# One mask for four token tiles, the dt series in portions over two passes, and two end tiles on GpSimd

## The chip, the cores and the metric

The kernel runs on one core of a Trainium2 chip. The core has five engines with an instruction queue each: TensorE (PE, matmuls and transposes), VectorE (DVE), ScalarE (ACT), GpSimd (POOL) and SyncE (SP, which here only issues transfers). They work side by side and wait for each other through semaphores. The metric is the device time of one execution in microseconds (us). PE's clock has two levels, 2.4 and 1.2 GHz; the profile gives the granted clock of a stretch as a share of the higher one.

## The reference

The input is 64 sequences of 32 tokens with 512 channels. Two blocks follow each other, and each adds its result to x.

```python
# block 1: conditional mixing, then a Mamba-2-like attention
att = softmax(mlp(cond))                         # 64 x 8
h   = einsum('boi,bih->boh', att @ weight, x) + (att @ bias_k)[:, :, None]
gate, xBC, dt = split(h @ in_proj_w.T)           # 4096, 6144, 64 columns
x_, B, C = split(silu(causal_conv4(xBC) + conv_bias))
dt  = softplus(dt + dt_bias)                     # 64 heads of 64 channels
state = state * exp(dt * A) + (dt * x_) outer B  # step by step over 32 tokens
y   = state . C + x_ * D                         # 8 heads share one group's B and C
y   = group_rms_norm(y) * norm_weight * silu(gate)
x   = x + y @ out_proj_w.T
# block 2: grouped convolution of 9 taps, then a masked dense layer
z     = conv9(x) + context + bias
hits  = softmax(z @ centroids.T / 0.1) > 0.01
keep  = any(hits, axis=1)[:, None] & any(hits, axis=0)[assignments][None, :]
x     = x + where(keep, z @ ffn_weight.T + ffn_bias, 0)
```

## The kernel before, in words

The 2048 tokens are 16 token tiles of 128, four sequences each. Four token tiles make a block. The scan over 32 tokens is written as products: for each head, Y = (G * L) applied to dt * x, where G is B times C for each pair of tokens of a sequence, and L the decay between them, masked to earlier tokens of the same sequence.

The main loop has 32 stages and a tail (`stage`, n from 0 to 32; L792). A stage is one group of eight heads for one block; even and odd stages alternate between two blocks, and the first 16 stages treat blocks 0 and 1, the last 16 blocks 2 and 3. In a stage ten projections (m from 0 to 9; `proj`, L456) make B (m = 0), C (m = 1), four tiles of x (m = 2 to 5) and four of the gate. A projection is 12 matmuls of 512 columns (L474), since numbers are split into a high and a low part and three products are kept. ACT evicts it from PSUM (`evac`, L479), DVE runs three taps of the causal convolution (`taps`, L501), and ACT the Silu (`silu`, L515). All engines' queues are filled by hand, in the order in which this loop calls the helpers; each engine works its own queue strictly in order. A `wait` in a queue therefore holds up all that is behind it on that engine.

Around the projections stand, on PE's queue:
- `A(n, i)` (L574), for each of the four token tiles i, behind projections 7, 8, 9 and the next stage's 0: four transposes of x (L585) and the product G of that tile (L589, 128 x 128, in the bank PG). A waits for `dtx` of the tile before, because the transposes share one PSUM bank (PT). DVE answers with `A_dve` (L592): `dtx` (L599), and two multiplies of G's diagonal halves by a mask (L607 on, `gmt`), then with `M_dve` (L611), the masked product.
- `Y(n, i)` (L621): 64 short products (L636), tiles 0 and 1 at the end of the stage, 2 and 3 at m = 2 of the next one.
- `O` (L716, matmuls L733) with the output weights and `S` (L697), for the stage before. On the other engines `y_dve`, `y_act`, `y_pool` (L641 to L690) and `add_out` (L738) belong to them.

A new block of tokens comes in at stages 0, 15 and 16 (`block_at`). There the stage also carries, for each of the block's four token tiles, the build of its mixing weights (`X_dve`, L328 to L338, three multiplies on DVE), the product (`X_pe`, L342, L352) and the split into xh (ACT) and xl (DVE, L366), at m = 1 to 4; and behind projection 6 the product that gives dt (`D_pe`, L372). The dt series (`D_chain`, L387) makes softplus of it: four operations and an Exp on ACT (L405 to L410), then 12 short steps on DVE (L412 to L426 and on), each waiting for the one before, on two halves of a PSUM bank and two tiles in SBUF. How many entries of the series are issued at each m is in the tuples `pace0` (stage 0) and `pace` (L780). All of it is issued by the end of the same stage, seven entries at m = 7, six at m = 8, ahead of `A_dve` of these projections' successors. `DT_pe` (L433, four transposes at L438) and `DT_split` (L440) turn the result behind the last Y of the stage.

In stage 0 DVE also makes the weights of the dt product (`dt_weights`) and the side inputs of block 2 (`side_inputs`), and PE their context product (`context_pe`, L291).

Block 2 (`second`) runs in steps over 16 token tiles: `conv2` (L995), `ffn` (L1044) and their operations. Its dense results of tiles 0 to 9 are kept with x already added; those of tiles 10 to 15 (`LATE` = 10) are computed at the end. `rsel` (L1149) is the mask of columns on all rows. At the end DVE selects for tiles 0 to 9 (`finish`, L1161: a predicated copy). For tiles 10 to 15 DVE takes them from PSUM and masks them and POOL adds (`finish_late`, L1168, L1173, L1176). SP stores each.

Of the kernel before, what the change touches and what calls it, by code (L numbers as in the profile page):

```python
# [56 lines left out]
def adaln_attn_ffn_kernel(nc, x, emb, gin, b2, wbank, biask, w_in, w_dt, w_out, prm, cst, cw4, ctxw,  # L57
                          w_ffn, b_ffn, asg, x2s, out):
    ctx = ExitStack()
    with ctx:  # L60
# [36 lines left out]
        gmt = sb("gmt", [128, 2, 64])  # L97
# [193 lines left out]
        def context_pe():  # L291
            pe.wait("ld_cx", 0)
            pe.wait("mx", 0)
            pe.op(lambda e: e.matmul(PS[:, PY[0], 128:192], yq[:, 0:128], eT, start=True, stop=True), "cx", 0)

        def side_inputs():
# [5 lines left out]
            dve.op(lambda e: e.tensor_tensor(cxt, PS[:, PY[0], 128:192].rearrange("p (t b) -> p t b", b=4),  # L302
# [66 lines left out]
        def D_bank(b):  # L369
            return PT if b == 0 else PY[0]  # L370
# [16 lines left out]
        def D_chain(b):  # L387
            d, x = PS[:, D_bank(b), 0:256], PS[:, D_bank(b), 256:512]
# [9 lines left out]
            def first():  # L398
                act.wait("D", b)
                if b >= 1:  # L400
                    act.wait("DT", b - 1)
                for r in range(2):
                    act.op(lambda e, r=r: e.activation(da[64 * r:64 * r + 64, :], PS[0:64, D_bank(b), 256 * r:256 * r + 256],
                                                       ACT.Abs, bias=bias), "dv", (b, r))
                for r in (1, 0):  # L405
                    act.op(lambda e, r=r: e.activation(d[64 * r:64 * r + 64, :], PS[0:64, D_bank(b), 256 * r:256 * r + 256],
                                                       ACT.Relu, bias=bias), "dre", (b, r))
                act.wait("dv", (b, 1))
                act.wait("dre", (b, 1))
                act.op(lambda e: e.activation(x, da[:, :], ACT.Exp, scale=-1.0), "de", b)  # L410
                dve.wait("de", b)
                step(lambda e: e.tensor_scalar(da[:, :], x, 2.0, None, ALU.add))  # L412

            def plus_max():
                dve.wait("dre", (b, 0))
# [15 lines left out]
            return [first] + [lambda fn=fn: step(fn) for fn in fns] + [plus_max, last]  # L431
# [83 lines left out]
        def silu(n, m):  # L515
            z = 6 * n + m
            act.wait("tap", (n, m, 2))
            if m < 2:
                if n >= 1:
                    act.wait("G", (n - 1, 3))  # L520
# [31 lines left out]
        def seg(n):  # L552
# [5 lines left out]
            for r in range(2):  # L558
                if n >= 1:
# [14 lines left out]
        def A(n, i):  # L574
            z, a = 4 * n + i, 128 * i
            if z == 0:
                pe.wait("dsp", 0)
# [6 lines left out]
            for j in range(4):  # L584
                fn = lambda e, j=j: e.transpose(PS[:, PT, 128 * j:128 * j + 128], xs[:, j, a:a + 128], ident)  # L585
                pe.op(fn, "T", (n, i)) if j == 3 else pe.op(fn)
            pe.wait(*shared[0])
            shared[0] = ("Gm", (n, i))
            pe.op(lambda e: e.matmul(PS[:, PG, 128 * (i % 2):128 * (i % 2) + 128], Bs[:, a:a + 128], Cs[:, a:a + 128],  # L589
                                     start=True, stop=True), "G", (n, i))  # L590

        def A_dve(n, i):  # L592
# [9 lines left out]
            dve.wait("G", (n, i))  # L602
            if z >= 2:
                dve.wait("M", divmod(z - 2, 4))
            for q in range(2):
                p, c = slice(64 * q, 64 * q + 64), 64 * q
                fn = lambda e, p=p, c=c: e.tensor_tensor(gmt[p, r, :], PS[p, PG, 128 * r + c:128 * r + c + 64],  # L607
                                                         C[p, C_GM + c:C_GM + c + 64], ALU.mult)
                dve.op(fn, "Gm", (n, i)) if q else dve.op(fn)

        def M_dve(n, i):  # L611
            r = i % 2
            if i >= 2 or n >= 1:
                dve.wait("Y", divmod(4 * n + i - 2, 4))
            dve.wait("L", (n, i // 2))
            dve.wait("Gm", (n, i))
            dve.op(lambda e: e.tensor_tensor(
                Mb[:, r], bc(Lt[:, 256 * i:256 * i + 256].rearrange("p (h o t) -> p h o t", h=8, o=1), 128, 8, 2, 32),
                bc(gmt[:, r, :].rearrange("p (o q t) -> p o q t", o=1, q=2), 128, 8, 2, 32), ALU.mult), "M", (n, i))

        def Y(n, i):  # L621
# [5 lines left out]
            if i == 0:  # L627
# [3 lines left out]
                if n in block_at:  # L631
                    pe.wait("dsp", block_at[n])
# [83 lines left out]
        def O(n, i):  # L716
# [10 lines left out]
            if i == 0 and n in block_at:  # L727
                pe.wait("ah", block_at[n])
                pe.wait("alo", block_at[n])
# [28 lines left out]
        for T in range(4):  # L758
# [6 lines left out]
            if T == 1:  # L765
                X_dve(3)
            if T >= 1:
                X_split(T)
                split_w_hi(0, T)
        context_pe()  # L770
# [5 lines left out]
        dt_weights()  # L776
        decay_rates()
        side_inputs()

        pace0 = (0, 7, 6, 0, 0, 0, 0, 7, 6, 0)  # L780
        pace = (0, 0, 0, 0, 0, 0, 0, 7, 6, 0)
        block_at = {0: 1, 15: 2, 16: 3}

        def X_tile(T, n):
            free = [{4: ("cxm", 0), 5: ("xl", 1), 6: ("xl", 2), 7: ("xl", 4)}.get(T, ("xl", T - 1))]
# [5 lines left out]

        def stage(n):  # L792
            real, prev = n < NS, n >= 1
            b = block_at.get(n)
            chain = D_chain(0) if n == 0 else []
            for m in range(10 if real else 7):

                lag = 1
                if b is not None and 0 <= m - lag <= 3:
                    X_dve(4 * b + m - lag)  # L800
                if prev:
# [6 lines left out]
                    for i in {0: (0,), 1: (1,), 3: (2, 3)}.get(m, ()):  # L808
                        y_dve(n - 1, i)
# [7 lines left out]
                if real:  # L817
                    if m == 6:
                        av(n)
                    if m == 9:  # L820
                        for go in chain:
                            go()
                        chain = []
# [36 lines left out]
                if n == 0 and m == 5:  # L860
                    DT_pe(0, [("xl", 5)])
                    DT_split(0)
                if b is not None:
                    if 1 <= m - lag <= 4:
                        X_tile(4 * b + m - 1 - lag, n)
                    if m == 6:
                        D_pe(b, [("acc", (n - 1, 2))] if n >= 1 else [("xl", 7)])
                        chain.extend(D_chain(b))
                if prev:
                    if m == 2:  # L870
                        Y(n - 1, 2)
                        Y(n - 1, 3)
                    for i in at("O"):
                        O(n - 1, i)
                        S(n - 1, i)
                if real:
# [58 lines left out]
        LATE = 10  # L935
# [139 lines left out]
        def ffn_ops(T):  # L1075
# [60 lines left out]
        for T in range(LATE, LATE + 2):  # L1136
            ffn(T, 0)
# [131 lines left out]
```

How the kernel before makes its waits and increments, by code:

```python
    def emit(self, eng, sems):  # L43
        seen = {}
        for it in self.items:
            if it[0] == "wait":
                v = self.book[it[1]][it[2]]
                if seen.get(it[1], 0) < v:
                    eng.wait_ge(sems[it[1]], v)
                    seen[it[1]] = v
            else:
                ins = it[1](eng)
                if it[2] is not None:
                    ins.then_inc(sems[it[2]], it[3])
```

## Time and profile before

| | |
|---|---|
| time, median of 3 runs | 1677.97 us (1677.83 to 1679.43) |
| the profiled execution | 1678.95 us, of which its span 1677.2 us |
| busy, share of the span | PE 97%, PEld 78%, DVE 66%, ACT 51%, POOL 47% |
| mean granted clock of PE | 0.991 |
| chain that ended last, by engine | PE 43%, issue 6%, POOL 3%, DVE 2%, ACT 1% |
| costliest group | projections (L474), 3 x 1280 matmuls, 393 to 413 ns each |
| DMA | 93.01 MB, mean 55 GB/s |

The page is read from the top: the share of each engine's busy time first, then the 40 slices of the span, in which PE shows 9 nearly everywhere. Matmuls overlap, so that the mean of one (393 ns) is longer than the distance to the next. A share is a mean over stages that differ; the rows below therefore go by stages, and a stage starts with the first product of its projection 0.

### The profile page before, as it was taken

How to read it: one execution, taken by the hardware profiler on the slowest of the kernel's cores; microseconds unless marked ns; L12 is line 12 of the kernel's file. 1: busy time of each engine (PE TensorE's matmuls, PEld its weight loads, DVE VectorE, ACT ScalarE, POOL GpSimd, SP SyncE). 2: the span in 40 equal slices, each digit the busy share in tenths (PEclk: the TensorE clock that was granted, in tenths of full speed). 3: DMA queues.
4: the chain of work that ended last, by engine and by line, in shares of the span. 5: the costliest groups of instructions: out<-in, count | busy, mean ns of one | idle time of the engine just before them, and what ended most of it. 6: DMA issues, size and time to landing. Idle time of an engine off the chain costs nothing.

```text
span 1677.2 us, 30511 instructions
## 1 busy us (share of the span) xinstructions
PE 1632.7 (97%) x11725; PEld 1316.0 (78%) x11725; DVE 1102.4 (66%) x1998; ACT 857.6 (51%) x1377; POOL 784.1 (47%) x762
## 2 busy tenths in 40 slices
PE   8899999999999999999999999999999999998996
PEld 6688888888888888877788888888888888886665
DVE  7867667666766566676676667666667667664456
ACT  4655545555555555445545555555555545554221
POOL 4364645555463636444254554546364645544101
PEclk9999999999999999999999999999999999999999
DMA  6111102011111111010012201111111102016772
GB/s 201 34 57 33 39 19 64 26 51 39 45 45 39 51 33 57 13 52 26 20 51 71 62 28 51 39 41 49 32 57 33 48 17 61 23 47 145 162 156 101
DMA packets 50288, 93.01 MB, mean 55 GB/s; under 512 B 5664, under 2 KB 6304, under 8 KB 50144
## 3 DMA queue, kind: packets, MB, share of 16 engines
q1 hardware_dynamic: 50144, 91.06, 18.8%
q8 instruction: 94, 1.54, 0.4%
q14 instruction: 50, 0.41, 0.1%
HBM read 82.59 MB, written 8.45 MB: 54 GB/s over the span
## 4 chain that ended last, share of the span: by engine, by line
PE 43%; issue 6%; POOL 3%; DVE 2%; ACT 1%; POOLq 0%; DVEq 0%
PE PS L474 22%; PE PS L733 9%; PE PS L1059 2%; PE PS L1005 2%; PE PS L636 2%; PE PS L585 1%; PE PS L697 1%; POOL yl L690 1%; PE PS L589 1%; POOL ysum L684 1%; PE PS L563 0%; PE PS L1024 0%; PE PS L356 0%; POOL yss L688 0%; POOL rs L714 0%
## 5 line engine op out<-in xcount | busy, mean ns | idle before, releaser
L474 PE MATMUL PS<-xh,wh 128*128 128x512 f32 x1280 | 528.9, 413 | 0.3 <-DVE xl L366 0.3
L474 PE MATMUL PS<-xh,wl 128*128 128x512 f32 x1280 | 503.0, 393 | 0.0
L474 PE MATMUL PS<-xl,wh 128*128 128x512 f32 x1280 | 500.9, 391 | 0.0
L509 DVE SCALAR_TENSOR_TENSOR cb<-PS,P,cb 128x496 f32<-128x496 f32 (+2 forms) x576 | 412.8, 717 | 74.4 <-ACT cb L495 59.7
L182 POOL TENSOR_TENSOR wl<-rw,wh 128x512 fp32r<-128x512 f32 x160 | 206.7, 1292 | 176.2 <-ACT wh L177 156.9
L474 PEld LDWEIGHTS PS<-xh,wl 128*128 128x128 f32 x1280 | 240.9, 188 | 54.7
L474 PEld LDWEIGHTS PS<-xh,wh 128*128 128x128 f32 x1280 | 241.8, 189 | 46.4 <-ACT wh L177 0.7
L684 POOL TENSOR_TENSOR ysum<-yq 128x256 f32<-128x256 f32 x128 | 95.4, 745 | 385.9 <-ACT yq L672 385.9
L474 PEld LDWEIGHTS PS<-xl,wh 128*128 128x128 f32 x1280 | 242.2, 189 | 42.6
L495 ACT ACTIVATE cb<-PS,P 128x512 f32<-128x512 f32 x192 | 149.3, 778 | 203.3 <-PE PS L474 201.5
L733 PE MATMUL PS<-oh,yh 128*128 128x512 f32 x512 | 202.6, 396 | 6.2 <-POOL yl L690 5.5
L733 PE MATMUL PS<-ol,yh 128*128 128x512 f32 x512 | 201.6, 394 | 0.0
L733 PE MATMUL PS<-oh,yl 128*128 128x512 f32 x512 | 201.3, 393 | 0.0
L690 POOL TENSOR_TENSOR yl<-yg,yh 128x512 fp32r<-128x512 f32 x128 | 194.3, 1518 | 12.5 <-ACT yh L677 12.4
L672 ACT ACTIVATE yq<-y 128x512 f32<-128x512 f32 x128 | 81.0, 633 | 213.0 <-DVE y L653 206.4
L714 POOL TENSOR_TENSOR rs<-vr,mh 128x1 f32<-128x1 f32 x128 | 70.4, 550 | 208.8 <-DVE vr L705 208.8
L746 DVE SCALAR_TENSOR_TENSOR acc<-PS,rs,acc 128x512 f32<-128x512 f32 x128 | 96.1, 751 | 91.9 <-issue 61.8
L599 DVE TENSOR_TENSOR dtx<-PS,dtt 128x512 f32<-128x512 f32 x128 | 88.0, 687 | 97.6 <-PE PS L585 97.6
L661 DVE TENSOR_TENSOR yg<-y,big 128x512 f32<-128x512 f32 x128 | 103.8, 811 | 72.4 <-POOL yl L690 69.1
L499 ACT ACTIVATE big<-PS 128x512 f32<-128x512 f32 x128 | 76.3, 596 | 125.7 <-PE PS L474 125.3
L529 ACT ACTIVATE big<-cb 128x512 f32<-128x512 f32 x192 | 119.4, 622 | 31.3 <-DVE cb L509 31.3
L653 DVE TENSOR_TENSOR y<-PS,big 128x512 f32<-128x512 f32 x128 | 87.5, 684 | 69.4 <-PE PS L636 69.4
(187 smaller groups left out, 2299.1 us busy)
## 6 DMA issues: line engine op xcount, KB each, us to landing
rw<-in_w_in SPq DMA_DIRECT2D x160, 256.0 KB, 2.7
ro<-in_w_out SPq DMA_DIRECT2D x64, 256.0 KB, 2.8
wh<-x2s SPq DMA_DIRECT2D x32, 258.5 KB, 4.9
wl<-x2s SPq DMA_DIRECT2D x32, 258.5 KB, 5.0
x2s<-acc SPq DMA_DIRECT2D x16, 260.0 KB, 4.3
out_x<-acc SPq DMA_DIRECT2D x16, 256.0 KB, 2.3
acc<-in_x SPq DMA_DIRECT2D x3, 1024.0 KB, 10.0
acc<-in_x SPq DMA_DIRECT2D x4, 256.0 KB, 4.4
```

The costliest lines, as they stand in the source:

```text
L182: pool.op(lambda e: e.tensor_tensor(wl[:, m, :], rw[:, q % RW, :], f(wh[:, m, :]), ALU.subtract), "w_lo", (u, m))
L474: fn = lambda e, k=k, w=w, v=v, i=i: e.matmul(PS[:, bank, :], w[:, m, 128 * k:128 * k + 128], v[:, k, a:a + 512], start=(i == 0), stop=(i ...
L495: act.op(lambda e: e.activation(cb[:, z % 2, :], PS[:, bank, :], ACT.Identity, bias=P[:, P_CB + c:P_CB + c + 1], scale=P[:, P_CW + 4 * c + ...
L509: dve.op(lambda e, d=d, w=w: e.scalar_tensor_tensor(out=cv[:, :, d:32], in0=pv[:, :, 0:32 - d], scalar=w, in1=cv[:, :, d:32], op0=ALU.mult ...
L529: act.op(lambda e: e.activation(dst, cb[:, z % 2, :], ACT.Silu), "silu", (n, m))
L599: dve.op(lambda e: e.tensor_tensor(dtx[:, r, :].rearrange("p (h c) -> p h c", h=8), PS[:, PT, :].rearrange("p (h c) -> p h c", h=8), bc(dt ...
L653: dve.op(lambda e: e.tensor_tensor(y[:, r, :].rearrange("p (j q t) -> p j q t", j=4, q=2), PS[:, PY[0]:PY[0] + 2, 256 * r:256 * r + 256].r ...
L661: dve.op(lambda e: e.tensor_tensor(yg[:, :].rearrange("p (j t) -> p j t", j=4), y[:, r, :].rearrange("p (j t) -> p j t", j=4), gate[:, :, ...
L684: pool.op(lambda e: e.tensor_tensor(ysum[:, :], yq[:, 0:256], yq[:, 256:512], ALU.add), "ys1", (n, i))
L690: pool.op(lambda e: e.tensor_tensor(yl[:, r, :], yg[:, :], f(yh[:, r, :]), ALU.subtract), "yl", (n, i))
L733: fn = lambda e, j=j, v=v, w=w, q=q: e.matmul(PS[:, PO[i], :], v[:, r, 128 * j:128 * j + 128], w[:, j, :], start=(q == 0), stop=(q == 11))
L746: dve.op(lambda e: e.scalar_tensor_tensor(out=acc[:, T, 4:516], in0=PS[:, PO[i], :], scalar=rs[:, i:i + 1], in1=acc[:, T, 4:516], op0=ALU. ...
```

## The change

- `A` no longer makes G. `G_all(n)` makes it for all four token tiles at once, behind the second pair of Y at m = 2 and ahead of projection 3: 16 products of 32 x 32, one for each sequence, put side by side in four column tiles of one bank. It waits for the Silu of B and C. `G_mask(n)` is one multiply on DVE for all four (128 x 256), at m = 3, ahead of the second pair of y. Silu's wait for G and M's for the mask go by stage now.
- The dt product always goes to bank PT; the series keeps its two other tiles in SBUF (`pb`) in place of PSUM. The series is issued in portions: one entry at m = 7, four at 8, four at 9, and the rest at m = 2 to 4 of the next stage (for the series of block 0, at m = 1 to 4 of stage 0). `DT_pe` and `DT_split` come at m = 5 of the next stage; the seg product there waits for them, and in place of "series done" A and Y wait for the Relu and for xl alone.
- The weight builds of the first two token tiles of a block come in the stage before (m = 6, 7), the others at m = 3 and 4; in stage 0 the first two come at m = 1.
- `dt_weights` goes to the setup, ahead of the first stage; `context_pe` and `side_inputs` go into stage 0 (m = 5 and 6, bank PG).
- At the end two tiles (`APART` = 2: tiles 0 and 1) keep their dense result without x. A second product `rsel2` and a copy on ACT bring the mask of columns into SBUF (`rows`), and POOL multiplies and adds. `rsel` comes behind the first late output product, not behind the third. The order of finishing is 2, 3, tile 0 apart, 4, 5, tile 1 apart, then the late tiles 10 to 15 with 6 to 9 in turn.

```diff
 def D_bank(b):
-    return PT if b == 0 else PY[0]
+    return PT
 def D_chain(b):
-    d, x = PS[:, D_bank(b), 0:256], PS[:, D_bank(b), 256:512]
+    d, x = pb[:, 0:256], pb[:, 256:512]
...
     act.op(lambda e: e.activation(x, da[:, :], ACT.Exp, scale=-1.0), "de", b)
+def add_two():
     dve.wait("de", b)
     step(lambda e: e.tensor_scalar(da[:, :], x, 2.0, None, ALU.add))
...
-    return [first] + [lambda fn=fn: step(fn) for fn in fns] + [plus_max, last]
+    return [first, add_two] + [lambda fn=fn: step(fn) for fn in fns] + [plus_max, last]
 def seg(n):
+    if r == 0 and n - 1 in block_at:
+        pe.wait("ah", block_at[n - 1])
+        pe.wait("alo", block_at[n - 1])
 def A(n, i):
-    if z == 0:
-        pe.wait("dsp", 0)
+    if i == 0 and n in block_at:
+        pe.wait("dre", (block_at[n], 1))
...
+def G_all(n):
+    pe.wait("silu", (n, 0))
+    pe.wait("silu", (n, 1))
     pe.wait(*shared[0])
-    shared[0] = ("Gm", (n, i))
-    pe.op(lambda e: e.matmul(PS[:, PG, 128 * (i % 2):128 * (i % 2) + 128], Bs[:, a:a + 128], Cs[:, a:a + 128],
-                             start=True, stop=True), "G", (n, i))
+    shared[0] = ("Gm", n)
+    for i in range(4):
+        for q in range(4):
+            a = 128 * i + 32 * q
+            fn = lambda e, i=i, q=q, a=a: e.matmul(PS[32 * q:32 * q + 32, PG, 32 * i:32 * i + 32], Bs[:, a:a + 32],
+                                                   Cs[:, a:a + 32], start=True, stop=True)
+            pe.op(fn, "G", n) if i == 3 and q == 3 else pe.op(fn)
+def G_mask(n):
+    dve.wait("G", n)
+    if n >= 1:
+        dve.wait("M", (n - 1, 3))
+    dve.op(lambda e: e.tensor_tensor(
+        gmt[:, :, :].rearrange("p i (q t) -> p i q t", q=2),
+        bc(PS[:, PG, 0:128].rearrange("p (i o t) -> p i o t", i=4, o=1), 128, 4, 2, 32),
+        bc(C[:, C_GM:C_GM + 64].rearrange("p (o q t) -> p o q t", o=1, q=2), 128, 4, 2, 32), ALU.mult), "Gm", n)
 def A_dve(n, i):
...
-    dve.wait("G", (n, i))
-    for q in range(2):
-        p, c = slice(64 * q, 64 * q + 64), 64 * q
-        fn = lambda e, p=p, c=c: e.tensor_tensor(gmt[p, r, :], PS[p, PG, 128 * r + c:128 * r + c + 64],
-                                                 C[p, C_GM + c:C_GM + c + 64], ALU.mult)
 def Y(n, i):
-    if n in block_at:
-        pe.wait("dsp", block_at[n])
+    else:
+        pe.wait("xl", 7)
...
-pace0 = (0, 7, 6, 0, 0, 0, 0, 7, 6, 0)
-pace = (0, 0, 0, 0, 0, 0, 0, 7, 6, 0)
+pace0 = (0, 4, 3, 3, 3, 0, 0, 1, 4, 4)
+pace = (0, 0, 1, 1, 3, 0, 0, 1, 4, 4)
 def stage(n):
-    if b is not None and 0 <= m - lag <= 3:
-        X_dve(4 * b + m - lag)
+    if n == 0 and m == 1:
+        X_dve(4)
+        X_dve(5)
+    if n + 1 in block_at and n >= 1 and m in (6, 7):
+        X_dve(4 * block_at[n + 1] + m - 6)
+    if b is not None and m in (3, 4):
+        X_dve(4 * b + m - 1)
...
+    if n - 1 in block_at and m == 5:
+        DT_pe(block_at[n - 1], [("acc", (n - 1, 1))])
+        DT_split(block_at[n - 1])
...
-    D_pe(b, [("acc", (n - 1, 2))] if n >= 1 else [("xl", 7)])
+    D_pe(b, [("xl", 4 * b + 3)])
...
+    if real and m == 2:
+        G_all(n)
+    if n == 0 and m == 5:
+        context_pe()
...
-    if b is not None:
-        DT_pe(b, [("L", (n, 0))])
-        DT_split(b)
...
+    if T < APART:
+        dve.op(lambda e: e.tensor_scalar(d, d, qs[:, T:T + 1], None, ALU.mult), "res", T)
+        return
...
+    pe.op(lambda e: e.matmul(PS[:, PT, :], csel, ohf, start=True, stop=True), "rsel2", 0)
+def finish_apart(T):
+    pool.op(lambda e: e.tensor_tensor(d, d, rows, ALU.mult), "sel2", T)
+    pool.wait("sel2", T)
+    pool.op(lambda e: e.tensor_tensor(acc[:, T, 4:516], acc[:, T, 4:516], d, ALU.add), "add", T)
+    stored(T, "add")
+rows = y[:, 0, :]
+act.op(lambda e: e.copy(rows, PS[:, PT, :]), "rows", 0)
```

## Rows read from the trace of the kernel before

**Rows 1.** The page, part 1: busy time, share of the span, instructions of each engine.

```profile
PE 1632.7 (97%) x11725; PEld 1316.0 (78%) x11725; DVE 1102.4 (66%) x1998; ACT 857.6 (51%) x1377; POOL 784.1 (47%) x762
```

**Rows 2.** Windows: length, busy us (instructions) of PE, PEld, DVE, ACT, POOL, PEclk, DMA.

```profile
24.00:60.00 36.00, 30.60 (x146) 22.95 (x147) 34.63 (x55) 18.21 (x33) 24.93 (x21) 1.00 0.18 52
...
748.00:751.40 3.40, 3.40 (x12) 2.92 (x12) 3.23 (x5) 0.59 (x1) 1.25 (x2) 0.50 0.36 105
...
781.30:843.70 62.40, 57.99 (x390) 45.27 (x389) 43.64 (x83) 31.00 (x49) 17.13 (x19) 0.97 0.08 22
...
843.70:889.97 46.27, 45.90 (x336) 37.57 (x334) 28.93 (x51) 26.64 (x44) 29.00 (x28) 1.00 0.28 88
```

**Rows 3.** Time line of PE, stages 16 and 17: start, us, operation, idle before.

```profile
830.30 0.60 PE L585 MATMUL PS<-C,big 128*128 128x128 f32 x4
...
836.40 0.86 PE L585 MATMUL PS<-C,big 128*128 128x128 f32 x4 [2.55 <-DVE dtx L599]
...
843.34 0.44 PE L438 MATMUL PS<-C,dr 128*128 128x128 f32 x2
...
843.75 0.48 PE L474 MATMUL PS<-xh,wh 128*128 128x512 f32 x1
...
881.28 0.60 PE L585 MATMUL PS<-C,big 128*128 128x128 f32 x4
```

**Rows 4.** Time line of DVE, stage 16.

```profile
830.57 0.42 DVE L412 TENSOR_SCALAR da<-PS 128x256 f32<-128x256 f32 x1 [4.35 <-ACT PS L410]
...
833.75 0.42 DVE L426 TENSOR_SCALAR dr<-PS 128x256 f32<-128x256 f32 x1
...
835.66 0.68 DVE L599 TENSOR_TENSOR dtx<-PS,dtt 128x512 f32<-128x512 f32 x1
```

**Rows 5.** Time line of ACT, stage 16.

```profile
834.98 1.08 ACT L572 ACTIVATE Lt<-PS 128x512 f32<-128x512 f32 x2
```

**Rows 6.** Time line of PE's weight loads (PEld), stage 18.

```profile
930.99 0.30 PEld L589 LDWEIGHTS PS<-big 128*128 128x128 f32 x2
...
931.21 0.19 PEld L474 LDWEIGHTS PS<-xh,wh 128*128 128x128 f32 x1
```

**Rows 7.** Time line of PE, stage 18.

```profile
902.02 1.16 PE L636 MATMUL PS<-big,dtx 64*64 64x64 f32 x64
903.11 0.50 PE L474 MATMUL PS<-xh,wh 128*128 128x512 f32 x1
```

**Rows 8.** Time line of ACT, stage 18.

```profile
902.13 0.78 ACT L495 ACTIVATE cb<-PS,P 128x512 f32<-128x512 f32 x1 [2.90 <-PE PS L474]
...
902.81 0.62 ACT L529 ACTIVATE big<-cb 128x512 f32<-128x512 f32 x1
```

**Rows 9.** Time line of PE, convolution near the end.

```profile
1584.28 2.78 PE L1005 MATMUL PS<-wh,w 128*32 128x512 f32 x24
```

**Rows 10.** Time line of PE, stage 15.

```profile
746.86 0.47 PE L352 MATMUL PS<-ab,xb 64*128 64x512 f32 x1 [1.56 <-DVE xl L366]
```

**Rows 11.** Time line of DVE, stage 0.

```profile
28.75 2.21 DVE L509 SCALAR_TENSOR_TENSOR cb<-PS,P,cb 128x496 f32<-128x496 f32 x3
...
38.79 2.09 DVE L333 TENSOR_TENSOR bd<-AW,C 128x128 f32<-128x128 f32 x1
...
40.81 0.28 DVE L338 TENSOR_TENSOR ab<-xb,C 64x128 fp32r<-64x128 f32 x1
...
42.29 0.40 DVE L427 SCALAR_TENSOR_TENSOR dr<-dr,PS 128x256 f32<-128x256 f32 x1
```

**Rows 12.** Time line of ACT, stage 0.

```profile
26.95 0.78 ACT L495 ACTIVATE cb<-PS,P 128x512 f32<-128x512 f32 x1 [1.44 <-PE PS L474]
```

**Rows 13.** Time line of POOL, stage 0.

```profile
38.37 2.37 POOL L266 TENSOR_TENSOR big<-big 128x1024 f32<-128x1024 f32 x1
```

**Rows 14.** Time line of POOL, the end.

```profile
1672.76 1.27 POOL L1176 TENSOR_TENSOR acc<-acc,dtx 128x512 f32<-128x512 f32 x1 [0.49 <-DVE dtx L1173]
```

**Rows 15.** Time line of PE, the end.

```profile
1658.99 1.12 PE L1149 MATMUL PS<-Lt,csel 64*128 64x512 f32 x2
```

More of the change, by code:

```diff
@@ L292, in context_pe @@
             pe.wait("ld_cx", 0)
-            pe.wait("mx", 0)
-            pe.op(lambda e: e.matmul(PS[:, PY[0], 128:192], yq[:, 0:128], eT, start=True, stop=True), "cx", 0)
+            pe.wait(*shared[0])
+            shared[0] = ("cxm", 0)
+            pe.op(lambda e: e.matmul(PS[:, PG, 128:192], yq[:, 0:128], eT, start=True, stop=True), "cx", 0)
         def side_inputs():
@@ L401, in first @@
                     act.wait("DT", b - 1)
+                else:
+                    act.wait("mix", 2)
                 for r in range(2):
@@ L414, in plus_max @@
             def plus_max():
-                dve.wait("dre", (b, 0))
+                dve.wait("dre", (b, 1))
                 step(lambda e: e.scalar_tensor_tensor(out=dr[:, :], in0=dr[:, :], scalar=2.0, in1=d, op0=ALU.mult, op1=ALU.add))
@@ L519, in silu @@
                 if n >= 1:
-                    act.wait("G", (n - 1, 3))
+                    act.wait("G", n - 1)
                 dst = (Bs, Cs)[m]
@@ L808, in stage @@
                     for i in {0: (0,), 1: (1,), 3: (2, 3)}.get(m, ()):
+                        if i == 2 and real:
+                            G_mask(n)
                         y_dve(n - 1, i)
@@ L817, in stage @@
                 if real:
+                    if m == 3 and not prev:
+                        G_mask(n)
                     if m == 6:
                         av(n)
[L820 to L823, printed above, removed]
+                        if n == 0:
+                            side_inputs()
                     if m == 8:
@@ L1134, in adaln_attn_ffn_kernel @@
             second(step)
-        for T in range(LATE, LATE + 2):
-            ffn(T, 0)
+        ffn(LATE, 0)
         pe.wait("pm", NT - 1)
@@ L1149, in adaln_attn_ffn_kernel @@
         pe.op(lambda e: e.matmul(PS[:, PG, :], csel, ohf, start=True, stop=True), "rsel", 0)
-        for T in range(LATE + 3, NT):
+        pe.op(lambda e: e.matmul(PS[:, PT, :], csel, ohf, start=True, stop=True), "rsel2", 0)
+        for T in range(LATE + 1, NT):
             ffn(T, 0)
@@ L1177, in finish_late @@
             stored(T, "add")
-        for T in range(4):
-            finish(T)
+        def finish_apart(T):
+            d = spots[T]
+            pool.wait("rows", 0)
+            pool.wait("res", T)
+            pool.wait(f"sx{T // 4}", 4 * (T // 4) + 3)
+            pool.op(lambda e: e.tensor_tensor(d, d, rows, ALU.mult), "sel2", T)
[3 more added lines that the diff above has]
+        rows = y[:, 0, :]
+        act.wait("rsel2", 0)
+        act.wait("yg", (end_n, 3))
+        act.op(lambda e: e.copy(rows, PS[:, PT, :]), "rows", 0)
+        finish(2)
+        finish(3)
+        finish_apart(0)
+        finish(4)
+        finish(5)
+        finish_apart(1)
         for T in range(LATE, NT):
             finish_late(T)
-            finish(T - LATE + 4)
+            if T < LATE + 4:
+                finish(T - LATE + 6)
         sp.wait("st", last_store[0])
```

38 lines of the change are left out of this document (17 added, 21 removed).

## The prediction

> **What bounds the kernel now.** I read the page first, then windows cut at the first product of a stage, then time lines. The page has TensorE (PE) busy for 97% and VectorE (DVE) for 66% [rows 1]; an ordinary even stage lasts 46.27 us with PE busy for 45.90 [rows 2]. So in an ordinary stage only what PE itself issues or waits for counts, and the 28.93 us of DVE there have room. Three stages are different: stage 16 lasts 62.40 us with PE busy for 57.99 (stages 15 and 0 show the same pattern), and from 24 to 60 us, inside stage 0, DVE is busy for 34.63 of 36.00 us [rows 2]: there DVE is the bound. I forecast from PE's gaps in these three places and from PE's own work in the others.
>
> **The dt series, second half of stages 0, 15 and 16.** In an ordinary stage the way from the first transposes (881.28 [rows 3]) to the next stage (889.97, the window's edge in rows 2) is 8.69 us. In stage 16 it is 843.75 - 830.30 = 13.45 [rows 3], 4.76 more; the same way is 2.92 longer in stage 15 and 4.72 in stage 0: 12.4 together. Cause: DVE waits 4.35 us for the Exp of the series, then runs seven of its steps, and only then dtx, possible since about 831, at 835.66 [rows 4]; PE waits for it until 836.40, 2.55 idle [rows 3], and runs at a lower clock behind that. After the change dtx of tile 0 goes first, then four steps (830.57 to 833.75 [rows 4], 3.2 us). The masked product of tile 0 waits for the exponentials of ScalarE (ACT), 834.98 + 1.08 for two, so the first at 835.6 [rows 5]; then dtx of tile 1 is through at 837.0, and PE comes there at 830.30 + 2 x 3.3 = 836.9. So the cover is just used up, with 0 to 0.3 left over each. Of the 12.4, 3 x 0.41 are the transposes of dt (843.34 to 843.75 [rows 3]), which only move to the next stage, ahead of an O, so they are paid there: gain 11.2 at best. If the rest of the series, which still stands in front of y, keeps a third, it is 7.5. I take **-11.0**.
>
> **B times C on PE, 32 stages.** Removed: four 128-column products G a stage. Each is two weight loads and two matmuls between the transposes and the next projection. Its first weight load starts at 930.99, the projection's at 931.21 [rows 6]: without G the projection's load takes that place, 0.22 us earlier. 4 x 0.22 = 0.88 a stage, 28.2 in all. Stages are PE bound there, so I count it whole.
>
> Added: one group of 16 products of 32 columns (32 matmul instructions) behind the second pair of Y and ahead of projection 3. It waits for the second Silu of the stage (C), which stands on ACT behind the eviction of projection 2. In the trace Y's 64 instructions go from 902.02 to 903.11, where projection 3 starts [rows 7]; the eviction starts at 902.13 and the Silu ends at 902.81 + 0.62 = 903.43 [rows 8]. With 0.06 to reach PE (dtx ends at 836.34, PE starts at 836.40 [rows 3, 4]) the group can start at 903.49: PE waits 0.38 that it doesn't wait now. Behind the waiting group stand projection 3 and all later PE work, so nothing hides it.
>
> The length of the group no row shows. From below: 24 matmuls of 512 columns on four 32-column tiles take 2.78 us [rows 9], 0.116 each; 32 columns are a sixteenth, 7 ns each, 0.23 for 32. From above: Y's instructions have 64 columns and take 17 ns each, changes of tile shape included [rows 7], 0.55 for 32. I take 0.45, nearer to Y, which like this group stands between full products. Net per ordinary stage: 0.38 + 0.45 - 0.88 = -0.05. In the 29 stages 1 to 14 and 17 to 31 this adds 29 x 0.83 = 24.1. In 15 and 16 a product of the next token tiles already stands in front, which covers the Silu, and the group's own 0.45 falls into a later wait of PE (below): 0. Stage 0 has its own term. Sum of G: 24.1 - 28.2 = **-4.1** (by the two bounds -10.5 to -1.2).
>
> *The Trainium skill, "TensorE: Matmul & The Clock Gate", section "Wait — 56ns, not 53.3ns?", says that the start of one matmul never follows the other by less than about 25 ns, however few columns it has. By that the group would take an estimated 0.8 us and the term would be +6. The 17 ns of Y [rows 7] speak against it for tiles side by side.*
>
> **The mask on DVE.** Eight 64x64 multiplies a stage become one of 128x256 from PSUM; dtx, twice as wide from PSUM, takes 0.68 [rows 4], so this one is below that. DVE has 17 us of room in a stage: 0. Where that room is gone (stages 0, 15, 16) the new one stands ahead of y and costs up to 0.5, in the next two terms.
>
> **First half of stages 15 and 16.** PE waits 1.56 us for xl of the second new tile [rows 10], which stands behind y, the evictions and the taps; stage 16 repeats it. Two of the four weight builds move to the stage before, about 0.8 less ahead of y (three operations like those of 0.28 in rows 11); mask, group and a step of the series put 0.4 to 0.9 back. So the wait ends about where it does now. In stage 15 it is followed by 3.40 us at 0.50 of the clock, 1.2 GHz [rows 2], which costs 1.7; with PE's idle stretch shortened by the group that may go, and it may come elsewhere. Between -1.7 and +1.7, I take **-0.8**.
>
> **First half of stage 0.** DVE is the bound [rows 2]. The side inputs leave it, but taps can't start before the first eviction, which ends at 27.73 [rows 12], where now they start at 28.75 [rows 11]: 1.0 gained. Against it: PE waits for the second Silu, the mask joins, and the series reads and writes pb in SBUF where it used PSUM. A multiply with both inputs in SBUF that starts at 38.79 takes 2.09 us [rows 11] and ends 0.14 after an operation of GpSimd (POOL) that runs from 38.37 for 2.37 [rows 13]; its like at 40.81 takes 0.28, and the series' step with a PSUM input at 42.29 0.40. POOL is busy for 24.93 of these 36 us [rows 2], most densely in the middle, where nine steps with only SBUF inputs would fall and now seven do, six of them from weight builds. At 1.1 (half of that POOL operation) nine waits are 10, where now DVE loses about 4: DVE's end comes some 5 later. Without these waits it comes 1 earlier. Bounds -1 to +7; I take **+4.0**.
>
> *"SBUF — State Buffer" of the Trainium skill, section "Who interferes with whom", has the rule: a DVE operation with two SBUF inputs and a GpSimd operation that reads SBUF exclude each other, the later one is fully blocked. The 2.09 agrees. By the rule this term is positive; without it the sum would be 5 lower.*
>
> **The end.** POOL's last add ends at 1672.76 + 1.27 = 1674.03 [rows 14] and starts the last store. The row mask's product moves ahead of two output products, from 1658.99 [rows 15] to about 1657.3, and a second one of its 1.06 us feeds ACT's copy: rows ready at about 1660.0. POOL then has 2 x 2 + 6 = 10 operations of 1.27 and 0.3 between them: 1673.0. DVE, which loses two of its selections and can start its share 1.7 earlier, is done before. The 16 stores stay 16; on SP those of tiles 4 and 5 now stand behind POOL's first sum, with time to spare. **-0.9** (-1.2 to 0).
>
> **Sum.** -11.0 - 4.1 - 0.8 + 4.0 - 0.9 = -12.8. The profiled execution took 1678.95 (span 1677.2): 1666.2. The median of the runs shown is 1.0 below it: 1665.
>
> **Rivals.**
> 1. *Slower: the four column tiles don't overlap for short products.* A single 32-column instruction would then take half of four times Y's 17 ns, 34 ns: 32 x 34 + 0.1 = 1.19 us, 0.74 above mine, 29 times: +21.5, so 1686. It decides from 0.89 us a group (12.8/29 above 0.45). For it: no row has 32 columns on PE's moving side. Against: rows 9, where four such tiles run side by side.
> 2. *A floor of 25 ns a matmul*, wherever it goes: 0.8 and 0.1 for the change of shape, +13, so 1678, no change. Against it Y's 17 ns. *The page named first has this floor.*
> 3. *The series stays in the way*: steps with SBUF inputs wait for POOL in the second halves too, two thirds of the 11 remain, stage 0 costs 5: 1665 + 7 + 1 = 1673. For it: POOL's splits in odd stages. Against: in the second half of stages 0 and 16 it has none to do.
> 4. *The portions do nothing*, since ACT's exponentials are late in any case: 1665 + 11 = 1676. Against: dtx was possible more than 4 us before it ran [rows 4].
>
> **Chances.** My forecast 0.73 (1655 to 1671 by its own terms, whose ends don't all fall on one side), rival 3 0.11, rival 4 0.05, rival 2 0.04, rival 1 0.07. The range 1655 to 1677 takes in rivals 3 and 4 and leaves out 1 and 2. 0.2% (3.4 us) is about what a measurement here tells from no change: faster 0.73 + 0.11 = 0.84, within it rivals 2 and 4, 0.09, slower 0.07.
>
> **What would show it.** The way from the last Y to projection 3 some 0.8 us longer in 29 stages, of which PE idles 0.38; transposes followed by a projection 0.22 sooner; no PE wait of over 0.5 us for dtx in stages 0, 15 and 16; the first transposes of stage 0 later than now; POOL's last add still the last before the end, DVE done before it. Wrong would be: a group longer than 0.9 us, waits for dtx that stay, or ordinary stages more than 0.3 us longer or shorter.

## The result and the profile after

The changed kernel takes 1662.94 us (median of 4 runs, 1660.19 to 1664.10) against 1677.96 of the kernel before; the ratio is 0.9906, 95% interval 0.9889 to 0.9923. The forecast was 1665 (1655 to 1677). The profiled execution took 1662.89, with a span of 1661.1: 16.1 below that of before, where the sum of the prediction was 12.8. The total is right, but by errors of both signs. By place, cut in the time lines of the two profiled executions at the first product of a stage and at the first transposes:

| place | before | after | change | prediction, put on this place |
|---|---|---|---|---|
| 27 ordinary stages (2 to 14, 18 to 31, the last up to the end of its projections) | 1233.2 | 1226.2 | -7.0 | -1.4 (27 x -0.05) |
| first transposes to next stage, in 0, 15, 16 | 38.5 | 25.0 | -13.5 | -14.2 (-11.0, -1.2 for the moved transposes, -2.0 of G) |
| stages 1 and 17 | 92.4 | 95.1 | +2.6 | +0.7 |
| first halves of 15 and 16 | 99.0 | 100.7 | +1.8 | -0.8 |
| first half of 0 | 41.3 | 44.6 | +3.3 | +4.0 |
| last projection to the end | 148.9 | 145.6 | -3.3 | -0.9 |

First the page's busy times, then windows of stage 16 and of stage 18 (columns as in [rows 2]), which answer to [rows 1, 2]:

```profile
PE 1619.4 (97%) x12495; PEld 1300.1 (78%) x12495; DVE 1066.9 (64%) x1772; ACT 857.0 (52%) x1378; POOL 780.9 (47%) x766
```

```profile
773.87:833.21 59.34, 57.54 (x418) 44.88 (x412) 42.12 (x69) 31.25 (x51) 19.89 (x20) 0.97 0.08 23
...
880.74:926.19 45.45, 45.11 (x363) 37.07 (x357) 31.06 (x47) 23.54 (x36) 18.26 (x19) 1.00 0.13 42
```

An ordinary stage is still PE bound: 45.11 busy of 45.45. Stage 16 is 3.1 shorter, though PE's busy time hardly fell.

**Second half of stage 16.** Time lines of PE, then DVE, which answer to [rows 3, 4]:

```profile
824.79 0.60 PE L592 MATMUL PS<-C,big 128*128 128x128 f32 x4
...
831.54 0.66 PE L592 MATMUL PS<-C,big 128*128 128x128 f32 x4 [0.19 <-DVE dtx L622]
...
833.21 0.50 PE L478 MATMUL PS<-xh,wh 128*128 128x512 f32 x1
```

```profile
825.42 0.69 DVE L622 TENSOR_TENSOR dtx<-PS,dtt 128x512 f32<-128x512 f32 x1 [1.85 <-PE PS L592]
826.03 0.28 DVE L416 TENSOR_SCALAR da<-pb 128x256 f32<-128x256 f32 x1
...
830.80 0.68 DVE L622 TENSOR_TENSOR dtx<-PS,dtt 128x512 f32<-128x512 f32 x1
```

dtx of tile 0 now runs before the series, not behind seven of its steps, and dtx of tile 1 ends at 831.48: PE still waits 0.19, where it waited 2.55 before. The way from the first transposes to the next stage is 8.42 (8.34 and 8.25 in stages 0 and 15).

**The group in stage 18.** PE, then ACT, which answer to [rows 7, 8]:

```profile
892.61 1.16 PE L650 MATMUL PS<-big,dtx 64*64 64x64 f32 x64
894.12 0.46 PE L602 MATMUL PS<-big 128*32 128x32 f32 x32 [0.34 <-ACT big L533]
894.50 0.50 PE L478 MATMUL PS<-xh,wh 128*128 128x512 f32 x1
```

```profile
892.72 0.78 ACT L499 ACTIVATE cb<-PS,P 128x512 f32<-128x512 f32 x1 [2.70 <-PE PS L478]
893.40 0.62 ACT L533 ACTIVATE big<-cb 128x512 f32<-128x512 f32 x1
```

Y's 64 products are through at 893.71 (1.09 after 892.61, as in other stages); the group waits for the Silu's end at 894.02 and starts at 894.12, 0.41 late. To the next projection it is 0.39 (12 ns for each of 32 instructions). Forecast were 0.38 and 0.45.

### The profile page after: what moved, and what is told of

Its sections match the earlier page's. It is cut to its first block, busy times and chain, and to the rows that moved or that the text cites. A ratio compares the mean times of both kernels' runs of the same rounds, so it can differ in the third digit from the quotient of the medians.

```text
span 1661.1 us, 31702 instructions
## 1 busy us (share of the span) xinstructions
PE 1619.4 (97%) x12495; PEld 1300.1 (78%) x12495; DVE 1066.9 (64%) x1772; ACT 857.0 (52%) x1378; POOL 780.9 (47%) x766
## 4 chain that ended last, share of the span: by engine, by line
PE 81%; issue 7%; ACT 4%; POOL 4%; DVE 3%; POOLq 0%; DVEq 0%
PE PS L478 47%; PE PS L744 19%; PE PS L592 3%; PE PS L1084 2%; PE PS L1030 2%; PE PS L650 2%; PE PS L711 2%; ACT big L533 1%; PE PS L357 1%; PE PS L602 1%; PE PS L570 1%; DVE cb L513 1%; POOL yl L704 1%; PE PS L571 1%; PE PS L206 1%
## 5 line engine op out<-in xcount | busy, mean ns | idle before, releaser
L478 PEld LDWEIGHTS PS<-xh,wh 128*128 128x128 f32 x1280 | 241.1, 188 | 46.2 <-ACT wh L177 1.0
L704 POOL TENSOR_TENSOR yl<-yg,yh 128x512 fp32r<-128x512 f32 x128 | 165.5, 1293 | 12.3 <-ACT yh L691 12.3
L691 ACT CAST yh<-yg 128x512 fp32r<-128x512 f32 x128 | 79.6, 622 | 88.6 <-DVE yg L675 72.7
```

The lines of the kernel that those rows point to most:

```text
L478: fn = lambda e, k=k, w=w, v=v, i=i: e.matmul(PS[:, bank, :], w[:, m, 128 * k:128 * k + 128], v[:, k, a:a + 512], start=(i == 0), stop=(i ...
L704: pool.op(lambda e: e.tensor_tensor(yl[:, r, :], yg[:, :], f(yh[:, r, :]), ALU.subtract), "yl", (n, i))
```

## Experiments

**G by itself, and everything but G.** In the changed kernel the even ordinary stages are 0.5 shorter each, where I forecast 0.05. Here and below, PE's seg product (L570) sums in each stage the decays that POOL writes in two operands, high and low (L551), ahead of ACT's exponentials. The first kernel is that of before with the group alone; the second the changed one with the old G.

```diff
 # kernel before: A() without G; at m = 2 behind Y
+if real and m == 2:
+    G_all(n)
...
 # changed kernel: G_all, G_mask out; A() and A_dve() as before
```

> The kernel before with the group of products and its one mask alone (series, weight builds and end as before). Theory 1, from the two traces: an ordinary stage pays 0.39 for the group and 0.41 of waiting for the second Silu and saves 0.89; in the 14 even ordinary stages about 0.44 more is saved, because the added time falls into a wait of TensorE for GpSimd's second decay operand, which stood ahead of the seg product before. So odd stages -0.05, even stages -0.5 each, the three special stages about -0.4 each: 7 to 9 us faster, 1669 to 1671. Theory 2, my prediction's term: -0.05 in every ordinary stage, 4 us faster, 1674. Theory 3: the gain of the even stages came from the series or the setup; then even and odd stages here show the same change.

> The changed kernel with the old four products G inside A and the two multiplies of the mask (series, weight builds and end as changed). Theory 1: loses the 7 to 9 us of the group, 1670 to 1672; TensorE's wait ahead of the seg product of the even stages is back (0.4). Theory 2: loses 4 us, 1667. Stages 1 and 17 stay longer than other odd stages by 2 us, since that comes from the end of the series.

G alone: 1670.40 against 1678.18, ratio 0.9953 (0.9941 to 0.9966), 7.8 faster; even stages 45.46 in the mean (45.94 before), odd ones 45.44 (45.52). All but G: 1668.36, ratio 0.9949 (0.9936 to 0.9963); even stages 45.95, odd 45.52. (Stage 14, where two weight builds now stand, is left out of the means of the changed kernels' even stages: it gained nothing, 46.03 for 45.98.) By the stages theory 1 holds: the group, not the series, makes the even stages 0.5 shorter. The median of the second kernel alone doesn't decide, since it lies between the theories' 1667 and 1670; and its stages 1 and 17 are 48.6, 3.1 above the other odd ones, where I expected 2. What had stood there is seen when the old G is back. Stage 18 of that kernel, POOL and PE's weight loads, then the same place of the changed kernel, POOL and PE:

```profile
915.21 2.36 POOL L551 TENSOR_TENSOR yl<-al,C 128x1024 fp32r<-128x1024 f32 x1
```

```profile
917.64 0.19 PEld L570 LDWEIGHTS PS<-yh,uf 128*128 128x128 f32 x1 [0.60 <-issue]
```

```profile
914.67 2.36 POOL L551 TENSOR_TENSOR yl<-al,C 128x1024 fp32r<-128x1024 f32 x1
```

```profile
917.23 0.40 PE L570 MATMUL PS<-yh,uf 128*128 128x512 f32 x1
```

With the old G, PE's seg product (L570) loads its weights 0.07 after POOL has finished its second decay operand (917.57): PE waits for POOL, some 0.4, though the row says "issue". In the changed kernel PE comes some 0.6 later in its stage to this place (0.8 for the group, less 0.22 for the G that stood behind projection 0), POOL is just done (917.03), and the wait is gone. So half of the group's 0.8 fell into a wait that was there.

**The Silu ahead of the eviction, and POOL's operand ahead of its rs.**

```diff
 # ordinary stages, m == 2
+silu(n, 1)
 evac(n, m)
-silu(n, m - 1)
```

> The changed kernel with one pair turned on ScalarE's queue in the ordinary stages: the second Silu (C) ahead of the eviction of projection 2. Its input is ready about 1 us before that eviction starts. Theory 1: the 0.41 us that TensorE waits ahead of the group goes in all ordinary stages; odd stages are 0.41 shorter, even stages stay as they are, since the wait for GpSimd's second decay operand comes back there: 15 x 0.41, 6 us faster, 1657. Theory 2: nothing takes its place, 29 x 0.41, 12 us faster, 1651. Theory 3: the wait isn't the Silu's place in the queue: 1663, no change.

```diff
 # and on POOL's queue, m == 6
+av(n, 0)           # high operand
 rstd_pool(n - 1, 3)
-av(n)
+av(n, 1)           # low operand
```

> The changed kernel with the second Silu ahead of the eviction (as in the run before) and GpSimd's first decay operand ahead of its rs of the last token tile, in place of both operands behind it. Theory 1: the second operand then ends about 0.9 earlier, so that TensorE no longer waits ahead of the seg product of the even stages: even stages go from 45.40 to 45.05, odd ones stay at 45.05; 13 x 0.35, 4 to 5 us below the kernel with the Silu alone, 1649 to 1651. Theory 2: rs, 1.9 us later, makes the last add_out late, for which the second seg product waits, and even and odd stages lose up to 0.5: 1654 to 1668.

The first: 1653.97, ratio 0.9854 (0.9837 to 0.9872). Odd stages 45.06, even stages 45.40, as theory 1 said; by the stages' sum that is 5.6. The 9 between the medians lies halfway to theory 2 and doesn't decide: this kernel's profiled execution also reaches stage 0 earlier by 2.7 and has no stretch of low clock in stage 15 (1.6), and both change from one execution to another (under "The end", below). The group follows Y at once in stage 18 (PE):

```profile
884.73 1.16 PE L650 MATMUL PS<-big,dtx 64*64 64x64 f32 x64
885.82 0.46 PE L602 MATMUL PS<-big 128*32 128x32 f32 x32
```

and the wait for POOL is back in the same stage, since PE is early again (PEld):

```profile
909.20 0.19 PEld L570 LDWEIGHTS PS<-yh,uf 128*128 128x128 f32 x1 [0.52 <-issue]
```

With POOL's order changed too, 1652.13, ratio 0.9845 (0.9831 to 0.9858): even stages 45.05, like the odd ones. Six stages (12, 13, 18, 19, 26, 27) are 0.3 to 0.5 longer there. In stage 18 it is ACT that is late (ACT):

```profile
913.62 0.72 ACT L189 ACTIVATE oh<-ro,P 128x512 fp32r<-128x512 f32 x1 [2.24 <-DMA ro<-in_w_out]
```

Its split of the output weights waits 2.24 for their transfer, 0.49 in stage 20. The exponentials behind it come 1.7 later, with them DVE's dtx, and PE waits 0.28 for that (0.31 in stages 13, 19 and 27).

**The order of the 16 products.**

```diff
-for i in range(4):
-    for q in range(4):      # q: column tile
+for q in range(4):
+    for i in range(4):
```

> The changed kernel with the 16 products of the group in another order: the four products of one column tile behind each other, in place of going round the four tiles. In the changed kernel the group of 32 instructions takes 0.39 us, 12 ns each. Theory 1, the tiles overlap: a product of one tile alone takes longer and is hidden by its neighbours in other tiles; then the new order shows it, the group takes 0.8 us or more, and 29 stages are 0.4 or more longer, 12 us slower, 1675. Theory 2: 12 ns is the distance of one small matmul to the next, in whatever tile: group 0.39, no change, 1663.

1672.68, ratio 0.9971 (0.9960 to 0.9982): 9.7 above the changed kernel's median. Each ordinary stage is 0.4 longer (45.85), and this is PE in stage 18:

```profile
945.34 0.87 PE L602 MATMUL PS<-big 128*32 128x32 f32 x32 [0.34 <-ACT big L533]
946.14 0.50 PE L478 MATMUL PS<-xh,wh 128*128 128x512 f32 x1
```

The group takes 0.80, 25 ns for each instruction, where going round the column tiles it takes 0.39. *By the floor of about 25 ns in the Trainium skill's "TensorE: Matmul & The Clock Gate", section "Wait — 56ns, not 53.3ns?", the group could, by an estimate (32 times 25 ns), not be shorter than 0.8: this run agrees, for products of one column tile behind each other; round four tiles the trace shows half of it, and the measurement decides.*

**Stages 1 and 17.** They became 1.3 longer each. In stage 17 (DVE, POOL, PE of the changed kernel):

```profile
859.26 1.36 DVE L420 SCALAR_TENSOR_TENSOR dr<-dr,pb 128x256 f32<-128x256 f32 x1
```

```profile
859.05 1.30 POOL L182 TENSOR_TENSOR wl<-rw,wh 128x512 fp32r<-128x512 f32 x1 [0.56 <-ACT wh L177]
...
867.82 1.92 POOL L551 TENSOR_TENSOR yh<-ah,C 128x1024 fp32r<-128x1024 f32 x1
869.69 1.92 POOL L551 TENSOR_TENSOR yl<-al,C 128x1024 fp32r<-128x1024 f32 x1
```

```profile
871.71 0.47 PE L570 MATMUL PS<-yh,uf 128*128 128x512 f32 x1 [0.86 <-issue]
```

The last steps of the series hold up DVE's taps, these its variance, this the root that POOL makes of it (rs), and behind that stand the decay operands, which end at 871.61.

```diff
-pace = (0, 0, 1, 1, 3, 0, 0, 1, 4, 4)
+pace = (0, 0, 1, 4, 0, 0, 0, 1, 4, 4)
```

> The changed kernel with the last three steps of the series at m = 3 of the next stage, where VectorE waits 0.8 to 1.4 us for an eviction, in place of m = 4. Theory 1: in stages 1 and 17 the three steps and their wait for GpSimd (1.36 where 0.43 would do) make the taps, the variance, GpSimd's rs and with it the two decay operands late, which is the 0.9 us that TensorE waits ahead of the seg product; so these stages are 0.6 to 0.9 shorter each, stage 16 up to 0.5: 1 to 2 us in all, 1661 to 1662. Theory 2: the decay operands are late by the transposes and copies of dt themselves: no change, 1663.

1660.08, ratio 0.9898 (0.9885 to 0.9912). Stages 1 and 17 are 46.85 and 46.84, 0.7 shorter each: theory 1. The gain of up to 0.5 in stage 16 did not come: 57.75, and 57.78 in old_end below, with the old pace and no low clock there either. The totals alone could not have told this from no change. DVE, with the step free of POOL, and PE, whose wait is nearly gone:

```profile
850.09 0.43 DVE L420 SCALAR_TENSOR_TENSOR dr<-dr,pb 128x256 f32<-128x256 f32 x1
```

```profile
866.19 0.47 PE L570 MATMUL PS<-yh,uf 128*128 128x512 f32 x1
```

**POOL's builds out of the series' way in stage 0.** The changed kernel, DVE and POOL, which answer to [rows 11, 13]:

```profile
38.69 2.37 DVE L430 TENSOR_SCALAR dr<-pb 128x256 f32<-128x256 f32 x1
...
45.19 2.05 DVE L334 TENSOR_TENSOR bd<-AW,C 128x128 f32<-128x128 f32 x1
```

```profile
38.33 2.58 POOL L266 TENSOR_TENSOR big<-big 128x1024 f32<-128x1024 f32 x1
...
44.73 2.37 POOL L266 TENSOR_TENSOR big<-big 128x1024 f32<-128x1024 f32 x1
```

```diff
-if n == 0 and m in (2, 3):
-    mixing_weights_pool(m)
+if n == 0 and m == 3:
+    pool.wait("dsp", 0)          # series done
+    mixing_weights_pool(2)
+    mixing_weights_pool(3)
```

> The changed kernel with GpSimd's two builds of later mixing weights (each about 5 us, in stage 0 at m = 2 and 3) held until the dt series of block 0 is done. Theory 1, exclusion: the series' steps that read only SBUF and the weight builds on VectorE are long because GpSimd works at the same time (2.37 and 2.05 us against 0.29 and 0.28 when it doesn't); without it the step L430 takes 0.3, the two long weight builds 0.3 each, VectorE is 5 to 6 us earlier, and stage 0 is 3 to 4 us shorter, as far as GpSimd's decay operands then allow: 1659 to 1660. Theory 2: the steps are long of themselves, or VectorE is bound by its own work: the rows stay and stage 0 is the same or, with GpSimd's work now ahead of the decay operands, up to 4 longer.

1661.70, ratio 0.9908 (0.9894 to 0.9921): no change that the medians show, but the rows change as theory 1 said (DVE, then ACT, POOL and PE further on in stage 0):

```profile
38.97 0.29 DVE L430 TENSOR_SCALAR dr<-pb 128x256 f32<-128x256 f32 x1
...
42.37 0.28 DVE L334 TENSOR_TENSOR bd<-AW,C 128x128 f32<-128x128 f32 x1
```

```profile
60.34 0.60 ACT L503 ACTIVATE big<-PS 128x512 f32<-128x512 f32 x1 [3.67 <-POOL AW L272]
```

```profile
64.58 2.35 POOL L551 TENSOR_TENSOR yl<-al,C 128x1024 fp32r<-128x1024 f32 x1
```

```profile
67.03 0.77 PE L570 MATMUL PS<-yh,uf 128*128 128x512 f32 x1 [3.20 <-issue]
```

The series ends 28.1 after the first product of the stage (in the changed kernel 32.3; both by L425), and the gain is given back further on. ACT's eviction of the gate waits 3.67 for POOL's last build, and POOL's decay operands, now behind both builds, end at 66.93: PE idles 3.20 ahead of the seg product. That is theory 2's price. Stage 0 takes 55.70 here, 52.98 and 55.04 in two executions of the changed kernel, so it is not shorter.

**The end.**

```diff
-LATE, APART = 10, 2
+LATE = 10
 # finish, rsel and their order as in the kernel before
```

> The changed kernel with the end of before (all selections of tiles 0 to 9 on VectorE, one row mask behind the third late product). Theory 1, from the traces (27.5 us from the last of the transposes to the end before, 25.6 now): 1.9 us slower, 1664.8. Theory 2, my prediction's term: 0.9 slower, 1663.8.

1660.63, ratio 0.9893 (0.9879 to 0.9906): not slower than the changed kernel, against both theories. The changed kernel was run again beside others:

> The changed kernel itself, unchanged, beside the other kernels of this call, as their comparison: 1660 to 1664. Stages other than 0, 15, 16 and the end within 0.1 us of the first profile; where those four differ, it is by stretches at half the clock, which fall elsewhere from one execution to the next.

1662.92 (1657.30 to 1663.62), ratio 0.9906 (0.9891 to 0.9921). Single executions of this one kernel span 7 us, so that 2 us don't show in these medians.

The profiled execution of old_end is 4.6 shorter than that of the changed kernel although its last projection to the end is 2.1 longer: stages 0, 15 and 16 are 4.1 shorter together (15 and 16 without their stretch of low clock), and stage 0 begins at 21.2 us, not at 23.9. That beginning changes from execution to execution, with the same set-up code in the changed kernel and all its variants: 21.2 to 21.7 in five of the fourteen profiled ones (no_g, old_end, silu_first, pace_early, mix_later), 23.7 to 24.3 in the others, the kernel before among them. In the set-up six equal products (L206) take PE 1.66 us in old_end and 2.93 in the changed kernel.

So the pair was run again on the fastest version (silu_av with the pace of pace_early):

> The changed kernel with the second Silu ahead of the eviction, GpSimd's first decay operand ahead of its last rs, and the last steps of the series at m = 3 of the next stage. The gains add up: 11 us of the first two (as in the run with both) and 1.4 of the third in stages 1 and 17: 1650 to 1651. Rival: the earlier operand takes the place of what the earlier steps gain, and stages 1 and 17 stay at 47.6: 1652.

> The same kernel with the end of before, to settle what the two tiles on GpSimd are worth. Theory 1, from the traces (from the last projection to the end 147.6 us with the old end, 145.6 with the new one): 2 us slower than the kernel above. Theory 2, from the medians so far (old end 17.5 below its kernel before, new end 15): the new end gains nothing or loses up to 2; then the order of finishing or the extra product gives back elsewhere what the trace shows.

1650.09, ratio 0.9832 (0.9819 to 0.9845): the gains add up, with stages 1 and 17 at 46.96 and 46.93. With the old end it is 1650.32, ratio 0.9837 (0.9823 to 0.9850). In the traces the way from the last of the block-2 transposes to the end of the span is 25.7 with the new end and 27.5 with the old one, as in the first pair (25.6 and 27.5). The trace shows 1.8; the medians show 0.2, and cannot tell 1.8 from nothing. Whether the new end makes the whole time shorter is therefore not shown. POOL at the end of the changed kernel, which answers to [rows 14]:

```profile
1645.90 1.31 POOL L1211 TENSOR_TENSOR big<-big,y 128x512 f32<-128x512 f32 x1 [86.61 <-ACT y L1219]
...
1651.17 4.99 POOL L1203 TENSOR_TENSOR acc<-acc,big 128x512 f32<-128x512 f32 x4
1656.11 2.49 POOL L1203 TENSOR_TENSOR acc<-acc,dtx 128x512 f32<-128x512 f32 x2
```

POOL's six late sums run back to back (7.4), where before five of the six waited 0.49 for DVE.

**One build alone held back, on the fastest version.**

```diff
 if n == 0 and m in (2, 3):
+    if m == 3:
+        pool.wait("dsp", 0)
     mixing_weights_pool(m)
```

> The same kernel as best with GpSimd's last build of mixing weights alone held until the series of block 0 is done. In the run with both builds held, VectorE was through with the series 4 us earlier, and ScalarE's first gate eviction then waited 3.7 us for GpSimd. Theory 1: with one build that wait goes (it ends about 4 us earlier on GpSimd) and half of the 4 us on VectorE is kept: stage 0 is 1 to 2 us shorter, 1648 to 1649. Theory 2: the decay operands behind it on GpSimd are late in its place: no change.

1646.61, ratio 0.9817 (0.9803 to 0.9830). Windows of stage 0, of the version without and with this edit:

```profile
24.17:79.18 55.01, 49.51 (x303) 37.49 (x303) 45.21 (x67) 32.07 (x53) 27.14 (x21) 0.91 0.19 59
```

```profile
24.08:73.68 49.60, 46.97 (x302) 35.21 (x302) 43.52 (x68) 32.41 (x53) 27.18 (x21) 0.97 0.21 65
```

Stage 0 is 5.4 shorter, more than forecast: PE also has one stretch of 3.4 at the lower clock in it where it had three (0.97 against 0.91 in the mean), which can make 3.4 of the 5.4 at most. It made less, by silu_av: its stage 0 is the same code as that without the edit, has one such stretch too, and is 54.03, so that some 4.4 are the edit's. This version beats both kernels: 16 us below the changed one, 31 below the one before.

## Why the prediction was right, and which steps were not

That the total came within a few us is partly luck. The ordinary stages gave 5.6 more than forecast and the end 2.4 more; the first halves of 15 and 16 gave 2.6 less, stages 1 and 17 1.9 less. The two mechanisms that carry the forecast, dtx ahead of the series and one group for four products, are shown.

**The dt series, -11.0.** The cause was right and the cover too: I reckoned 0 to 0.3 left of each wait and PE waits 0.19 in stage 16. The second halves give 13.5, of which 2.0 is G's share and 1.2 the moved transposes: 10.3 against 11.0. Part of it is clock: before, a stretch of 3.4 at half clock began in the second halves of stages 0 and 16, as with G alone; with the series in portions none began there in any profiled execution. By an estimate (half of 2 x 3.4) that is up to 3.4 of the 13.5. The step that failed is "only move to the next stage, ahead of an O, so they are paid there": behind the transposes hangs a chain of ACT, DVE and POOL to the seg product, late by 0.9 in stages 1 and 17, which became 1.3 longer each and not 0.35. I had priced what stood behind the moved instructions on PE's queue, not who waits for their result. Shown by pace_early, as far as 0.7 of each 0.9.

**B times C, -4.1.** The added terms were right to 0.1 (0.39 and 0.41 for 0.45 and 0.38), so was the saving: odd stages -0.08. The step that failed is "Stages are PE bound there, so I count it whole". In even stages PE had a wait of 0.4 for POOL further on, and time added ahead of a wait is not lost: they are 0.48 shorter, beyond the 0.3 that the prediction named as a sign of being wrong. G alone gives 7.8. The window of [rows 2] that I called an even ordinary stage is stage 17, an odd one and the one behind a new block (46.2, the other odd ones 45.5), in which this wait is short.

**The rivals.** The first (1.19 a group) and the second (0.8) did not come true; q_outer shows that the second would have, with another order of the two loops. The third is true of stage 17's steps, and small. The fourth is out.

**First halves of 15 and 16, -0.8.** Measured +1.8, of which 0.5 is dt's transposes in stage 16. The rest is mostly the clock: +0.2 in the second execution, where stage 15 has no stretch at half clock. In stage 15 the same wait of PE for xl stands in two executions of the changed kernel, without any difference in the code. The row of each (PE), and the window that begins 1.70 after its start:

```profile
742.80 0.46 PE L353 MATMUL PS<-ab,xb 64*128 64x512 f32 x1 [1.41 <-DVE xl L367]
```

```profile
744.50:748.00 3.50, 3.50 (x10) 2.73 (x10) 2.94 (x5) 0.58 (x1) 0.69 (x1) 0.51 0.25 75
```

```profile
745.16 0.46 PE L353 MATMUL PS<-ab,xb 64*128 64x512 f32 x1 [1.40 <-DVE xl L367]
```

```profile
746.86:750.36 3.50, 3.50 (x18) 2.92 (x18) 3.10 (x6) 0.59 (x1) 0.88 (x2) 1.00 0.32 75
```

Once a stretch near 0.5, 1.2 GHz, follows, once full clock. Stage 15 is 58.06 in the one and 56.50 in the other. In stage 16 such a stretch came in both executions (59.3), and none in that of pace_early (57.75). So the wait ended as I said, 1.8 lies just outside my bounds of 1.7 (1.3 without the transposes, which I had priced elsewhere), and the size was a matter of the execution.

**First half of stage 0, +4.0.** Measured +3.3, and +5.3 in the second execution of the same kernel. The size came true, the cause only in part. Windows of this half, before, changed kernel, silu_av (columns as in [rows 2]):

```profile
23.91:65.22 41.31, 35.91 (x169) 26.96 (x170) 35.23 (x55) 23.33 (x42) 27.31 (x21) 1.00 0.18 52
```

```profile
23.90:68.54 44.64, 40.11 (x202) 29.66 (x203) 38.23 (x55) 23.94 (x42) 27.00 (x21) 0.92 0.16 51
```

```profile
23.77:69.37 45.60, 38.58 (x203) 28.83 (x204) 38.20 (x55) 23.65 (x42) 27.22 (x21) 0.96 0.17 53
```

That POOL holds up DVE is shown by mix_later (2.37 to 0.29), and by best_mix3: at the same 0.96 of the clock this half is 41.58 there. That the series' steps in SBUF made the +3.3 is not shown: with G alone, the series still in PSUM, it is 44.71 too. In the changed kernel PE idles less than before (4.5, before 5.4) and runs at 0.92 of the clock; in silu_av it idles 7.0, at 0.96. How the time divides between waits for DVE and clock stays open. I had the exclusion for operations with two SBUF inputs; here a TENSOR_SCALAR with one was held too. *The Trainium skill, "SBUF — State Buffer", section "Who interferes with whom", names this form among those that can take the port pair shared with GpSimd; the trace agrees.*

**The end, -0.9.** Measured 1.9 behind the last transposes: POOL's start was as worked out, and its last sum ends 1.25 earlier against the transposes, where I had 1.0 (its operations leave no gap of 0.3). The other 0.6 I had not reckoned: from the last sum to the end of the span it is 2.5, before 3.1. Another 1.4 ahead of that is one stretch of low clock fewer.

## What to carry to other kernels

Time added to the bounding engine is lost only up to its next wait, so follow the engine through a whole period of the loop (here two stages) before you price an edit. A moved step is priced by the last one who waits for its result, on every engine that it goes through. Where two engines exclude each other, order their work by hand, and look at who needs the held one next.

## What the runs showed of the hardware

Products of 32 columns that go round four column tiles follow each other at 12 ns, those of one tile at 25 ns (32 instructions in 0.39 and 0.80 us). A VectorE operation of 0.29 us took 2.37 while GpSimd worked. The same wait of 1.4 us is followed by half clock in one execution and not in another, which is 1.6 us each time, and the first stage begins 2.7 us earlier in some executions than in others. Executions of one kernel differed by up to 7 us here, so steps of 1 to 2 us had to be read from the stages of the trace.
